# Picks by matmul in more chunks of all four layers, and in the high/low form in layers 0 and 3

## The reference, cut to what matters

```
layer 0: out = segment_sum( relu([h[dst], h[src], edge_attr_32] @ W1 + b1) @ W2 + b2, dst )
layer 1: a = softmax of edge_weight1 over the edges of each dst
         out = elu( segment_sum( h[src] * a, dst ) )
layer 2: out = segment_max( (h[dst] - h[src]) @ theta.T + theta_b + (h @ phi.T + phi_b)[src], dst )
layer 3: m = relu(relu([h[src], h[dst], edge_attr_16] @ W1 + b1) @ W2 + b2) @ W3 + b3
         out = h + segment_sum(m, dst) / max(count, 1)
```

## Time and profile before

| | |
|---|---|
| median of 3 runs | 8046.59 us (8039.53 to 8047.48) |
| profiled execution, its own time | 8039.29 us |
| its span, first to last instruction | 8036.4 us |
| busy: TensorE, GpSimd, VectorE, ScalarE | 6314.3, 6007.5, 4806.7, 2077.3 us |
| mean granted clock of TensorE | 0.877 |

### The profile page before, as it was taken

One profiled execution on the slowest core, in us unless ns is written; L12 is line 12 of the kernel. 1 busy time (PEld: TensorE's weight loads), 2 busy tenths in 40 slices (PEclk: granted clock), 3 DMA queues, 4 the chain that ended last, 5 costly groups with the idle time before them and its releaser, 6 DMA issues.

```text
span 8036.4 us, 78354 instructions
## 1 busy us (share of the span) xinstructions
PE 6314.3 (79%) x25061; PEld 4853.9 (60%) x25061; DVE 4806.7 (60%) x5969; ACT 2077.3 (26%) x4980; POOL 6007.5 (75%) x6324
## 2 busy tenths in 40 slices
PE   0399999999748888888578888888139988999982
PEld 0266666666537777777457777777026666666662
DVE  6366666666566666666766666666445555555553
ACT  5133333333212222222310000000014444444441
POOL 7777777777777777777767777777777777777776
PEclk9998988988769999999689999999568888888885
DMA  8344444444423334343223333333124444444442
GB/s 311 80 107 105 103 103 104 103 104 102 93 50 84 80 81 83 80 84 80 60 59 71 75 71 74 73 71 75 40 63 92 92 93 92 92 94 93 92 93 45
DMA packets 1047686, 712.72 MB, mean 89 GB/s; under 512 B 583794, under 2 KB 955028, under 8 KB 1047156
## 3 DMA queue, kind: packets, MB, share of 16 engines
q1 hardware_dynamic: 827552, 497.04, 22.2%
q0 software_dynamic: 203632, 168.38, 15.5%
q10 hardware_dynamic: 16100, 42.30, 1.4%
HBM read 469.72 MB, written 237.40 MB: 88 GB/s over the span
## 4 chain that ended last, share of the span: by engine, by line
POOL 52%; issue 17%; PE 2%; DVE 1%; DMA 1%; ACT 0%; POOLq 0%; DVEq 0%
POOL G L661 46%; POOL R L680 5%; POOL first_rows L622 1%; PE pOdd L885 1%; DVE S L1294 0%; PE pRows L960 0%; DVE onehot L1245 0%; ACT G L806 0%; DMA G<-table,idx 0%; DVE G L1257 0%; DMA G<-table,e_dst 0%; DMA prefix<-O 0%; PE pT L929 0%; PE pEven L941 0%; DMA R<-prefix,last_row 0%
## 5 line engine op out<-in xcount | busy, mean ns | idle before, releaser
L661 POOL DMA_INDIRECT G<-table,idx x3082 | 2913.9, 945 | 939.3 <-issue 932.9
L661 POOL DMA_INDIRECT G<-table,e_dst x2545 | 2408.0, 946 | 805.2 <-issue 772.3
L1183 DVE TENSOR_TENSOR_SCAN K<-mask_f,K,pT 48x512 f32<-48x512 bf16 x782 | 1005.2, 1285 | 1707.4 <-PE pT L929 1524.9
L960 PEld LDWEIGHTS pRows<-w,S 128*128 128x128 f32 x6256 | 1587.6, 326 | 401.4 <-issue 329.9
L885 PE MATMUL pOdd<-h_high,onehot 128*128 128x480 f32 (+1 forms) x3880 | 1562.8, 403 | 0.0
L885 PE MATMUL pOdd<-h_low,onehot 128*128 128x480 f32 (+1 forms) x3880 | 1517.6, 391 | 0.0
L960 PE MATMUL pRows<-w,S 128*128 128x48 f32 x6256 | 1446.1, 381 | 0.4 <-DVE S L1223 0.4
L929 PE MATMUL pT<-ident,G 128*112 128x128 f32 x3128 | 573.9, 314 | 921.9 <-DMA G<-table,idx 601.7
L929 PEld LDWEIGHTS pT<-ident,G 128*112 128x112 f32 x3128 | 416.4, 153 | 1405.4 <-DMA G<-table,idx 867.9
L1279 DVE STREAM_TRANSPOSE pT<-G 128x256 f32<-128x256 f32 x782 | 303.6, 433 | 949.6 <-DMA G<-table,e_dst 486.4
L885 PEld LDWEIGHTS pOdd<-h_high,onehot 128*128 128x128 f32 x3880 | 773.3, 199 | 140.9 <-issue 9.1
(11 more groups left out here) (188 smaller groups left out, 6383.9 us busy)
## 6 DMA issues: line engine op xcount, KB each, us to landing
mask_f<-same_row SPq DMA_DIRECT2D x392, 256.0 KB, 3.3
prefix<-O SPq DMA_DIRECT2D x194, 512.0 KB, 4.5
G<-first_rows SPq DMA_DIRECT2D x784, 96.0 KB
prefix<-O SPq DMA_DIRECT2D x390, 192.0 KB
G<-table,idx POOLq DMA_INDIRECT x3082
G<-table,e_dst POOLq DMA_INDIRECT x2545
first_rows<-zeros ACTq DMA_DIRECT2D x14, 2688.0 KB, 15.7
K<-in_ea_dram SPq DMA_DIRECT2D x588, 64.0 KB
```

The lines of the kernel that those rows point to most:

```text
L661: pool.indirect_dma_start(rows[:, slot, j, 0:widths[l]], None, table[l], bass.IndirectOffsetOnAxis(ap=at[:, n, j:j + 1], axis=0))\
L960: last = pe.matmul(o, s[:, :, j], (w2_0 if l == 0 else w3_3)[:, :], start=True, stop=True)
L1183: dve.tensor_tensor_scan(K[r, c.slot, :], mask_of(c, r), pT[c.slot % 2][r, :], K[r, (c.slot - 1) % RING, CHUNK - 1:CHUNK], ALU.mult, ALU.add)\
```

## The change

- Layers 1 and 2: every sixteenth chunk more is a pick, n % 16 = 12.
- Layer 0: picks at n = 13, 16, 19, ..., in the high/low form, each summed in three pieces (three chunks), with two one-hot tiles and two banks (`pH2`). The split of h into `h_high` and `h_low` is made by VectorE ahead of layer 0's loop, once the store of `decay_row` has landed (the tiles lie over it).
- Layer 3: picks at n = 14, 20, 26, ..., each summed in four pieces, with one one-hot tile and one bank, `pO[1]`; make_rows keeps only `pO[0]`. The split of h is made in the 14 parts, behind each h_made.
- The large negative number moves from the moving operand (bf16) into the stationary one (`minus_big`, bf16); the moving operand is 0 or 1 in fp8, for all picks in one tile. Several small tiles move to other places.
- SP loads the first two pick rows of a layer in its first step, and later ones ahead of their mark; it waits for the stored pick rows before layer 0.

```diff
-EDGE_PICK_SLOTS = (7,)
-EDGE_PICK_CYCLE = RING // len(EDGE_PICK_SLOTS)
-EDGE_PICK_FIRST = 2 * RING
+PICK_EXTRA = RING + 4
+EDGE_PICK_CYCLE = {0: 3, 3: 6}
+EDGE_PICK_LAG = {0: 5, 3: 6}
...
-    return [n for n in range(chunks) if n % RING in PICK_SLOTS]
+    return [n for n in range(chunks) if n % RING in PICK_SLOTS or n % (2 * RING) == PICK_EXTRA]
...
+def edge_picks(l, chunks):
+
+    return list(range(RING + EDGE_PICK_LAG[l], chunks, EDGE_PICK_CYCLE[l]))
...
+        edge_onehot = [over("e_prev", "e_w", "edge_onehot0", [P, PICK_GROUPS, P], f32r),
+                       over("H1", "S", "edge_onehot1", [P, PICK_GROUPS, P], f32r)]
+        unchosen = over("e_halves", "pick_id_i", "unchosen", [P, NP_ALL, SPAN], f8)
...
+        rows_bank = {0: pO, 3: [pO[0]]}
-        edge_sum = pH2[1]
+        edge_sum = {0: [pH2[1], pH2[0]], 3: [pO[1]]}
...
-            if l == 0 and n in EDGE_PICKS:
+            if l in MLP and n in EDGE_PICKS[l]:
                 return [j for j in range(TJ) if j != PICK_COLUMN]
...
+                    i = edge_pick_at(l, c.n + RING + EDGE_PICK_LAG[l] - 2)
+                    first = range(2) if c.n == 0 else []
+                    for k in [*first, *([i] if i is not None and i >= 2 else [])]:
+                        if k >= 2:
+                            sp.wait_ge(edges_marked, EDGE_PICKS_BEFORE[l] + k - 1)
+                        row = (FIRST_PICK[l] + k) * P
+                        sp.dma_start(mask_f[:, 2 * (k % 2), CHUNK:CHUNK + P],
...
+            def hide_unchosen(out, i):
+
+                pe.matmul(out[:, 0:SPAN * D], minus_big[:, :],
+                          unchosen[:, i, :].rearrange("p (s o) -> p s o", o=1).to_broadcast([P, SPAN, D]),
+                          start=True, stop=False)
+
+            def add_group(out, rows_of, g):
+
+                first, stop = g * SPAN, min((g + 1) * SPAN, B)
+                for part in (h_high, h_low):
+                    last = pe.matmul(out[:, 0:(stop - first) * D], rows_of[:, g, :],
+                                     part[:, first:stop, :].rearrange("p b d -> p (b d)"),
+                                     start=False, stop=g == PICK_GROUPS - 1 and part is h_low)
+                return last
...
-                    steps = EDGE_PICK_CYCLE - 2
+                    steps = min(EDGE_PICK_CYCLE[l], EDGE_PICK_LAG[l] - 2)
+                    for k in range(steps):
+                        i = edge_pick_at(l, c.n + RING + EDGE_PICK_LAG[l] - 2 - k)
...
-                          3: [(0, transpose_rows), (1, layer_1), (3, make_rows), (1, layer_2)]}[l]
+                          3: [(0, transpose_rows), (1, layer_1), (3, make_rows), (1, layer_2), (0, sum_edge_pick)]}[l]
...
-                if v == 1:
+                if v in (1, 3):
                     dve.wait_ge(h_made[v], q + 1)
+                    split_rows(bs)
...
-            link(part_of(slice(NP, NP_ALL), ALU.is_equal, edge_part))
-            link(part_of(slice(0, NP), ALU.not_equal, unchosen))
-            link(dve.tensor_scalar(unchosen, unchosen, -BIG, None, ALU.mult))
+            link(dve.tensor_tensor(
+                unchosen[:, :, :], pick_x[:, 1, :].rearrange("p (i o) -> p i o", o=1).to_broadcast([P, NP_ALL, SPAN]),
+                pick_id[:, 0:SPAN].rearrange("p (o s) -> p o s", o=1).to_broadcast([P, NP_ALL, SPAN]), ALU.not_equal,
+                saturate=False))
...
+                    dve.wait_ge(edges_summed, EDGE_PICKS_BEFORE[l] + i + 1)
+                    out = edge_sum[l][i % len(edge_sum[l])]
+                    dve.tensor_reduce(G[:, c.slot, PICK_COLUMN, 0:D],
+                                      out[:, 0:SPAN * D].rearrange("p (b d) -> p d b", d=D), AX, ALU.max)
...
+                if l == 0:
+                    dve.wait_ge(ex_stored, 32)
+                    dve.wait_ge(pick_stored, 16)
+                    dve.wait_ge(h_made[0], NQ)
+                    split_rows(slice(0, B))
...
-                stages = {0: [(0, choose_edge_pick), (0, spread_dst), (0, place_edge_pick), (0, mark_edge_pick), (2, scan)],
+                stages = {0: [(0, spread_dst), (0, place_edge_pick), (0, mark_edge_pick), (2, scan)],
...
-                          3: [(0, spread_dst), (2, scan)]}[l]
+                          3: [(0, spread_dst), (0, place_edge_pick), (0, mark_edge_pick), (2, scan)]}[l]
```

More of the change, by code:

```diff
@@ L122, in build @@
     NP = len(PICKS)
-    EDGE_PICKS = edge_picks(NCH)
-    NP_ALL = NP + len(EDGE_PICKS)
+    EDGE_PICKS = {l: edge_picks(l, NCH) for l in (0, 3)}
+    FIRST_PICK = {0: NP, 3: NP + len(EDGE_PICKS[0])}
+    NP_ALL = NP + len(EDGE_PICKS[0]) + len(EDGE_PICKS[3])
     SPAN = PICK_SPAN
@@ L186, in build @@
         ident = sb("ident", [P, P])
-        ident_h = sb("ident_h", [P, P], bf16)
+        minus_big = sb("minus_big", [P, P], bf16)
         w1_0 = sb("w1_0", [P, HID])
@@ L285, in build @@
         span_id = pH2[0][:, NODE_BLOCKS * WIDE:NODE_BLOCKS * WIDE + PICK_GROUPS]
+        edge_span_id = {l: [bank[:, SPAN * D:SPAN * D + PICK_GROUPS] for bank in edge_sum[l]] for l in (0, 3)}
+        assert SPAN * D + PICK_GROUPS <= CHUNK
         weights_in = sem("weights_in")
@@ L385, in build, with edge_pick_at, edge_row_count @@
         FIRST_DUO = {1: 0, 2: 2}
+        SPLIT_BEFORE = {0: 0, 1: 1, 2: 1 + NQ, 3: 2 + NQ}
+        EDGE_PICKS_BEFORE = {0: 0, 3: len(EDGE_PICKS[0])}
+        def edge_pick_at(l, n):
+            return EDGE_PICKS[l].index(n) if n in EDGE_PICKS[l] else None
+        def edge_row_count(l, i):
+            return 16 * (i // 2 + 1 + (sum(k % 2 == i % 2 for k in range(len(EDGE_PICKS[0]))) if l == 3 else 0))
         def gathers_of(l, n):
-            if l == 0 and n in EDGE_PICKS:
+            if l in MLP and n in EDGE_PICKS[l]:
                 return [j for j in range(TJ) if j != PICK_COLUMN]
@@ L456, in _ @@
             sp.wait_ge(G_zeroed, 1)
+            sp.wait_ge(pick_stored, 16)
             for l in range(4):
@@ L871, in multiply_h, with hide_unchosen_of @@
                         last.then_inc(hq_made, 1)
-            def hide_unchosen(d):
+            def hide_unchosen(out, i):
[9 more added lines that the diff above has]
+                return last
+            def hide_unchosen_of(d):
                 for k, i in enumerate(picks_of(d)):
-                    pe.matmul(pick_sum[d % 2][:, k, 0:SPAN * D], ident_h[:, :],
-                              unchosen[:, i, :].rearrange("p (s o) -> p s o", o=1).to_broadcast([P, SPAN, D]),
-                              start=True, stop=False)
+                    hide_unchosen(pick_sum[d % 2][:, k, :], i)
             def add_rows(d, g):
-                first, stop = g * SPAN, min((g + 1) * SPAN, B)
                 for k in range(len(picks_of(d))):
-                    for part in (h_high, h_low):
-                        last = pe.matmul(pick_sum[d % 2][:, k, 0:(stop - first) * D], onehot[:, d % 2 * 2 + k, g, :],
-                                         part[:, first:stop, :].rearrange("p b d -> p (b d)"),
-                                         start=False, stop=g == PICK_GROUPS - 1 and part is h_low)
+                    last = add_group(pick_sum[d % 2][:, k, :], onehot[:, d % 2 * 2 + k, :, :], g)
                 return last
@@ L953, in make_rows @@
                     pe.wait_ge(scanned[l], c.n + 1)
-                    if not (c.fixed and c.n < 2):
-                        pe.wait_ge(rows_copied[l], c.n - 1)
+                    banks = len(rows_bank[l])
+                    if c.n >= banks:
+                        pe.wait_ge(rows_copied[l], c.n - banks + 1)
                     w = widths[l]
@@ L1451 @@
     picks = src4[:, stream_picks(chunks), PICK_COLUMN]
-    edge_picks_of = src[:chunks * CHUNK].reshape(-1, P, TJ)[edge_picks(chunks), :, PICK_COLUMN].T
-    picks = np.concatenate([picks, edge_picks_of], 1)
+    by_chunk = src[:chunks * CHUNK].reshape(-1, P, TJ)[:, :, PICK_COLUMN].T
+    picks = np.concatenate([picks] + [by_chunk[:, edge_picks(l, chunks)] for l in (0, 3)], 1)
     arrays = {
```

114 lines of the change are left out of this document (43 added, 71 removed).

## The result

The changed kernel takes 7819.39 us in the median of 4 runs (7816.53 to 7821.56), the kernel before 8047.03 (8039.53 to 8048.41, 4 runs): a ratio of 0.9719 with a 95% interval of 0.9702 to 0.9736, 2.8% faster. 7832 had been forecast. The profiled execution took 7818.96 us, its span is 7817.2, 219.2 less than before. The mean granted clock of TensorE rose from 0.877 to 0.941.

A forecast was written before the change was run, and what follows sets the result against it. GpSimd's indirect gathers, 1.25 us each, were taken to bound the kernel: 8039.3 - 238.8 (191 gathers) + 8 (set-up) + 2 (splits) + 4 x 5 (losses) = 7830.5, stated as 7832 us. Range 7802 to 7885.

The forecast's parts named there:

- 0.1 for the mark: Layer 0: 0.1 us per pick, 13 us in all, put on TensorE for VectorE's mark between spread and scan.
- rival B: TensorE ends last in layer 0, needing 3.5% more: some 44 us with the tail, 7875 us in all; chance 0.26.
- the 97%: Layer 0: TensorE's 13.4 us per three chunks and a pick against GpSimd's 13.75; wrong if matmuls start over 0.22 us apart.
- A: The forecast's own case: GpSimd stays last everywhere, 7808 (no losses) to 7850 us; chance 0.68.
- The 5 us for a longer tail: Layer 0's end: 5 us charged because TensorE starts eight chunks behind and is still catching up; bounds 0 and 44.
- 8 us were forecast: Set-up before layer 0: VectorE's split stretches GpSimd's transfers by 6.3 us, the larger compare by 1.7; bounds 2 and 10.
- 30 us a layer less 5 of losses: Layers 1 and 2: 24 gathers fewer each at 1.25 us, GpSimd last, less 5 us of losses a layer.
- 78.8 less 5 of losses: Layer 3: 63 gathers fewer at 1.25 us, less 5 us for losses at late marks and the tail.
- the loss at late marks: Layer 3: waits at late marks, charged together with the tail at 5 us.
- The 14 splits ahead of the layer: Ahead of layer 3: splitting h in 14 parts may stretch GpSimd's transfers; 2 us taken, bounds 0 and 6.3.
- Rival C: TensorE's granted clock stays where it was though it is nearly solid: slower than before, 8060 us; chance 0.04.
- four times 5 us: Losses in the sum: 5 us for each of the four layers.

The follow-up runs named there:

- The two more hides: Changed kernel plus two more 480-column hiding matmuls, results overwritten, ahead of each of layer 0's 126 picks: 7853.95 us, 42.7 more than the change.
- The experiment with ScalarE: Changed kernel with the h_high copy ahead of layer 0 on ScalarE and layer 3's picks 5 and 6 chunks apart, in three pieces: 7800.07 us.
- the experiment with 27 of 32: Changed kernel with 27 instead of 26 picks per 32 chunks in layers 1 and 2: 7777.13 us, 34.1 less than the change.
- The change's second trace: Trace of the changed kernel run again unedited on another chip: 7811.21 us against 8039.64 for the kernel before, ratio 0.9715.

## Why the prediction was right

**GpSimd's gathers set the end, 1.25 us each.** By the loops in the traces, picks taken out cost 1.24 (layer 0), 1.23 (layers 1 and 2) and 1.24 us (layer 3) for each gather that came back. Picks added agree less closely: 26 gathers fewer shorten the two loops by 33.4 us, 1.28 each, and 6 fewer by 7.8, 1.31 each. The same loop differs by some 0.5 us between the traces of the experiments, and by up to 1.9 between the two traces of the change, which weighs on so few. In the loops of the changed kernel no wait of GpSimd for another engine is longer than its issue gap.

**TensorE in layer 0.** 13.4 us per three chunks were forecast, and 0.1 for the mark. Its timeline in the changed kernel (transposes, the start of a pick's last piece, a hiding matmul):

```profile
1210.49 0.60 PE L946 MATMUL pT<-ident,G 128*112 128x128 f32 x4
...
1213.51 0.46 PE L891 MATMUL pOdd<-h_high,edge_onehot 128*128 128x480 f32 x1
1213.81 0.38 PE L891 MATMUL pOdd<-h_low,edge_onehot 128*128 128x480 f32 x1
1214.03 0.37 PE L891 MATMUL pOdd<-h_high,edge_onehot 128*128 128x480 f32 x1
...
1218.22 0.37 PE L883 MATMUL pEven<-unchosen,minus_big 128*128 128x480 fp8e4 x1
...
1224.05 0.60 PE L946 MATMUL pT<-ident,G 128*112 128x128 f32 x4
```

13.56 us here and 13.63 for the next three (to 1237.69), 13.60 in the mean over the loop, where GpSimd's 11 gathers take 13.75. The room is 1.1%, where 3% were forecast. The first matmul of a piece that follows make_rows takes 0.30 us to the next one (1213.51 to 1213.81) instead of 0.22, twice in each pick. That is the going between the two forms which rival B named, and it makes about 0.17 of the 0.20 us missing from the 13.4. So one of the forecast's own signs came true: matmuls more than 0.22 us apart, by which the 97% would be wrong.

The forecast said that TensorE starts eight chunks behind and is not done catching up at the end; its own sum had it done at 2059, ahead of the last gather at 2083. It caught up at about 2000 us: from 328 to 2000 it waited 0.8 us in all for other engines and for no gather, from 2000 to 2095 7.5 us for gathers. So GpSimd set the rate from the start, as in A, while TensorE worked off its late start for nearly all of the layer, with next to no room, as in B. The chain of waits now runs through both, 47% POOL and 32% PE where it was 52 and 2:

```profile
POOL 47%; PE 32%; issue 16%; DVE 4%; DMA 2%; ACT 0%; POOLq 0%; SPq 0%; DVEq 0%; ACTq 0%
```

The 5 us for a longer tail, between bounds of 0 and 44, came out as 1.7 in the tail and 2 in the loop. The two more hides show that B's 44 were near: 3% more of TensorE's work cost 42.7 us. That the measured kernel fell on A's side hung on a reserve of some 11 us.

**Set-up.** 8 us were forecast (6.3 for the split, 1.7 for the compare), between 2 and 10; the first scan came 9.1 later. GpSimd's timeline, with 5.76 beside the compare, 3.22 beside the copy, 4.79 beside the subtract:

```profile
169.61 5.76 POOL L669 DMA_INDIRECT G<-table,idx  x1 [0.30 <-issue]
...
214.38 3.22 POOL L630 DMA_INDIRECT first_rows<-h,first_edge  x1 [0.30 <-issue]
217.90 4.79 POOL L630 DMA_INDIRECT first_rows<-h,first_edge  x1 [0.30 <-issue]
...
328.57 1.28 DVE L1199 TENSOR_TENSOR_SCAN K<-mask_f,K,pT 48x512 f32<-48x512 bf16 x1 [106.72 <-PE pT L946]
```

The copy and the subtract cost 3.22 + 4.79 - 1.94 = 6.1 us, about as forecast (6.3). The transfer beside the compare took 5.76 instead of 3.20, 2.6 more where 1.7 had been put; the last 0.4 us have no row. The experiment with ScalarE gave the copy's share back.
**Layers 1 and 2.** 30 us a layer less 5 of losses; the loops gave 28.3 and 28.6, so the losses were 1.7 and 1.4. The hiding matmul with an fp8 moving operand costs nothing: it takes 0.38 us alone and 0.58 for two, as the bf16 one did, and a two-pick duo takes 8.95 to 8.99 us, where it took 8.98. Of the 4% of room that the forecast had, the experiment with 27 of 32 used up nearly all.

**Layer 3.** 78.8 less 5 of losses; 76.5 came. 27.9 us were forecast for six chunks and a pick. In the changed kernel the hiding matmuls stand 28.30 us apart where TensorE waits for no gather, against 28.75 for GpSimd's 23 gathers:

```profile
6329.01 0.37 PE L883 MATMUL pRows<-unchosen,minus_big 128*128 128x480 fp8e4 x1
...
6350.58 1.94 PEld L978 LDWEIGHTS pRows<-w,S 128*128 128x128 f32 x8 [0.89 <-DVE S L1234]
...
6357.31 0.37 PE L883 MATMUL pRows<-unchosen,minus_big 128*128 128x480 fp8e4 x1
```

One of the six chunks took 4.35 us instead of 3.90: its make_rows waited for VectorE's scan, which stands behind the mark. That is the loss at late marks that the forecast named; it falls on TensorE, which has 1.6% of room left even so, and so costs no time. The version with 5 and 6 apart and picks in three pieces takes 27.87 for six chunks. The 14 splits ahead of the layer, 2 us between bounds of 0 and 6.3, cost nothing: 265.0 against 265.1 us.

**The clock.** Rival C, that it stays at 0.89 and 0.85, is out: 0.99 in both loops. (Its 8060 had a slip: the 74 us for layers 1 and 2 were window lengths less gathers, and the 48 gathers spared are 60 us, so 8074.) The versions with fewer picks had 0.84 and 0.87 where TensorE waited, at the same rate of gathers. The Trainium skill, "TensorE: Matmul & The Clock Gate", Part 1, that activity lifts the clock, is borne out by both pairs of windows.

**What was off.** The sum came 11.5 us too high (7830.5 against 7819.0). The losses had been put at four times 5 us without a row behind them; they were 2.0, 1.7, 1.4 and 2.3 in the loops and 1.7 + 1.7 in the transitions to layers 1 and 2, 10.8 in all. The splits gave back 2 more, set-up took 1, and the time around the span fell from 2.9 to 1.8 us. The change's second trace has losses of 0.5, 0.6, 0.0 and 0.5 us in the same loops and 1.0 and 1.1 in the transitions, so most of them are no more than the difference between two traces, and there was hardly anything to charge. The one term that was off in the mechanism was TensorE's need: 13.60 us for the 13.5 of layer 0 and 28.30 for the 27.9 of layer 3, 0.7 and 1.4% too low. It does not show in the time because GpSimd had still a little more to do in both, and in layer 0 that was close enough to call it luck. The sum by gathers alone, with what the rows priced (set-up 8, splits 2), would have been 7810.5.

## What to carry to other kernels

Where one engine issues back to back, the price of an instruction is its duration and its issue gap, and the count removed times that price is the gain, for as long as the engine that takes over the work needs less per period in a solid stretch. Take that need from back-to-back rows at full clock, not from busy shares: such sums held within 0.1 to 0.4 us a period, which is 0.1 to 1.5%. Where the room is 3%, that error can be half of it, so price the going between forms and the waits behind a late mark before counting on the rest. The waits that one imagines on top cost GpSimd's loops 1.4 to 2.3 us each in one trace and 0.0 to 0.6 in the other. And a busy share near 100% on the second engine does not say that it sets the end, since it may be catching up, but it does say that more work given to it is mostly paid: 42.7 of 54 us in layer 0.

## What the runs showed of the hardware

- The same program took 8039 to 8047 us on some chips and 9601 to 9612 on others. One kernel, traced on both kinds, has instructions of the same length (a gather 0.946 us on GpSimd, the scan of 48x512 1.285 and 1.286) and packets of GpSimd's queue that took the same time in all (1182 and 1203 us of the 16 engines); the waits are longer, up to 12.5 us for gathered rows. Which part of the chip is slower stays open.
- VectorE's tensor_tensor with both operands in SBUF, a 5060-element compare of 5.43 us or a 4704-element subtract of 5.06, holds up GpSimd's indirect DMA to 5.76 and 4.79 us; ScalarE's copy of the same 4704 elements, 4.12 us, leaves it at 0.97.
- A matmul of 480 columns with fp8 moving and bf16 stationary operands took 0.38 us alone and 0.58 for two, like the bf16 one.
- High/low matmuls of 480 columns start 0.22 us apart (1213.81 to 1214.03), but the first behind the fp32 matmuls of make_rows took 0.30 to the next.
